# A fused graph block on one core: score matmuls from two float32r parts in 64-row tiles, pairs of slots, and work moved between engines

## The reference

```python
h = relu(layernorm(x))                                  # first block
q, k, v = split(h @ W_qkv + b_qkv)                      # 8 heads of 16
scores = where(adj, q @ k.T / 4, -inf)                  # 512 x 512 per head
x = x + (softmax(scores) @ v) @ W_out + b_out
h = relu(layernorm(x))                                  # second block
zl, zg, v = h @ Wl, h @ Wg, h @ Wv
A_l = zero_diag(relu(cosine(zl, zl)))
A_g = zero_diag(exp(-|zg_i - zg_j|^2 / 2))
K_l, K_g = (row_normalise(A * adj) for A in (A_l, A_g))
x = x + ((0.9 * K_l + 0.1 * K_g) @ v) @ Wo
```

## Time and profile before

| | |
|---|---|
| median of three runs | 993.87 us |
| profiled execution: its own time | 983.95 us |
| profiled execution: span from first to last instruction | 981.9 us |
| TensorE matmuls busy | 876.3 us (89%) |
| TensorE weight loads busy | 496.0 us (51%) |
| VectorE busy | 760.2 us (77%) |
| ScalarE busy | 464.2 us (47%) |
| GpSimd busy | 170.6 us (17%) |
| DMA engines, mean share | 15.9% |
| mean granted TensorE clock | 0.989 |

### The profile page before, as it was taken

How to read it: one execution, slowest core, us unless ns; L and a number is a source line. 1 busy time by engine, 2 the same in 40 slices (tenths; PEclk the granted TensorE clock), 3 DMA queues, 4 the chain that set the end, 5 groups by cost and what they waited for, 6 DMA issues and landing times.

```text
span 981.9 us, 15346 instructions
## 1 busy us (share of the span) xinstructions
PE 876.3 (89%) x4991; PEld 496.0 (51%) x5075; DVE 760.2 (77%) x2461; ACT 464.2 (47%) x833; POOL 170.6 (17%) x224
## 2 busy tenths in 40 slices
PE   1479989999999999999999999999899999999987
PEld 1323345646455554645555464555546464655565
DVE  3767778788787878878688887878887887878465
ACT  1015555354545545364554545454454545455531
POOL 5312030121212021121202112120301212010110
PEclk9999989999999999999999999999999999999998
DMA  1331212030212103030211203021120302100000
GB/s 48 107 97 44 77 48 62 20 101 2 87 33 67 53 28 92 3 103 18 73 47 36 85 9 104 10 76 44 50 71 20 101 2 78 32 12 1 12 11 11
DMA packets 65534, 48.46 MB, mean 49 GB/s; under 512 B 10672, under 2 KB 65456, under 8 KB 65456
## 3 DMA queue, kind: packets, MB, share of 16 engines
q1 hardware_dynamic: 65456, 47.48, 15.9%
HBM read 30.28 MB, written 16.78 MB: 48 GB/s over the span
## 4 chain that ended last, share of the span: by engine, by line
PE 63%; DVE 25%; issue 4%; ACT 3%; SPq 2%; DMA 2%; POOL 1%; POOLq 0%; DVEq 0%; ACTq 0%
PE adj L516 11%; PE pv L509 10%; PE turned L497 8%; PE score L486 8%; PE adj L521 8%; PE turned L496 6%; DVE scrap L706 6%; PE work L527 6%; DVE adj_cos L841 3%; PE work L516 3%; DVE bn_sb L684 2%; DVE x_norm L693 2%; SPq L337 2%; PE work L616 1%; PE work L598 1%
## 5 line engine op out<-in xcount | busy, mean ns | idle before, releaser
L870 ACT ACTIVATE probs_t<-turned 128x512 f32<-128x512 f32 x512 | 306.0, 598 | 263.8 <-PE turned L497 251.3
L706 DVE CUSTOM_DVE_ANT_0 scrap<-score,mask_add 128x512 f32<-128x512 f32 x512 | 338.9, 683 | 30.3 <-PE score L486 29.4
L486 PE MATMUL score<-qk_rows 96*128 96x512 bf16 x512 | 202.6, 398 | 9.5 <-DVE neg_max L706 6.1
L497 PE MATMUL turned<-qk_rows 99*128 99x512 bf16 x512 | 195.5, 382 | 7.7 <-DMA qk_rows<-max_rows 2.9
L496 PE MATMUL turned<-bar_t,ident_b 128*128 128x512 bf16 x428 | 164.0, 383 | 0.8 <-DMA qk_rows<-max_rows 0.8
L509 PE MATMUL pv<-probs_t,v_cols 128*32 128x512 f32 x1024 | 137.3, 609 | 0.0
L486 PEld LDWEIGHTS score<-qk_rows 96*128 96x128 bf16 x512 | 50.2, 99 | 110.6 <-DVE neg_max L706 55.2
L497 PEld LDWEIGHTS turned<-qk_rows 99*128 99x128 bf16 x512 | 50.8, 99 | 58.8 <-issue 1.6
L428 POOL TENSOR_SCALAR var_eps<-moments 128x4 f32<-128x4 f32 x16 | 3.8, 237 | 427.6 <-DVE moments L688 427.6
L521 PEld LDWEIGHTS adj<-z,adj_cos 128*128 128x128 f32 x512 | 67.4, 193 | 10.7 <-DVE adj_cos L729 1.3
L521 PE MATMUL adj<-z,adj_cos 128*128 128x130 f32 x512 | 68.9, 278 | 1.5 <-DVE adj_cos L729 0.8
(11 more groups left out here) (107 smaller groups left out, 1102.3 us busy)
## 6 DMA issues: line engine op xcount, KB each, us to landing
qk_rows<-split_dram SPq DMA_DIRECT2D x384, 64.0 KB, 2.3
split_dram<-split SPq DMA_DIRECT2D x32, 384.0 KB, 2.6
x_sb<-in_x_dram SPq DMA_DIRECT2D x16, 256.0 KB, 2.9
out_dram<-out_sb SPq DMA_DIRECT2D x16, 256.0 KB, 2.3
qk_rows<-max_rows SPq DMA_DIRECT2D x96, 4.0 KB, 1.7
adj_sb<-in_adj_dram SPq DMA_DIRECT2D x1, 256.0 KB, 3.2
wqkv_sb<-in_L_gnn_W_qkv_dram SPq DMA_DIRECT2D x1, 192.0 KB, 2.7
bias_v<-in_L_gnn_b_qkv_dram SPq DMA_DIRECT2D x1, 64.0 KB, 2.8
```

The source lines that it names most:

```text
L486: pe.matmul(score_bank[u % 2][:, :], qk_rows[0:ROWS, b % 2, 0, h, t * P:(t + 1) * P], qk_rows[0:ROWS, b % 2, 1, h, :], start=True, stop=Tr ...
L497: pe.matmul(turned_bank[w % 2][:, :], qk_rows[0:ROWS + 3, b % 2, 1, h, j * P:(j + 1) * P], qk_rows[0:ROWS + 3, b % 2, 0, h, :], start=Fals ...
L706: dve.tensor_tensor_reduce(scrap[:, u % 2, :], score_bank[u % 2][:, :], mask_add[:, u % T, :], -1.0, 3.0e38, ALU.add, ALU.min, neg_max[:, ...
L870: act.activation(probs_t[:, k % 4, w % HG, :], turned_bank[w % 2][:, :], ACT.Exp, scale=SCALE).then_inc(probs_ready.sem, 1)
```

## The change

1. q and k are cut in two float32r parts rather than three bfloat16 ones (`Q_PARTS` 0,0,1 and `K_PARTS` 0,1,0): 48 rows rather than 96, four bytes each. Even heads stand from partition 0, odd heads from partition 64 (`ROW_HALVES`), and the matmuls name that 64-row tile (`tile_position`). GpSimd's two parts are gone; VectorE's residue is the second part. The maximum goes in two float32 rows; TensorE now transposes the maxima themselves, and ScalarE and VectorE each write one part from PSUM.
2. Score tiles and turned tiles are placed two at a time, at even slots: first the mask matmuls of both turned tiles, then score, turned, score, turned. The order of tiles is changed so that neighbouring slots are neighbouring heads.
3. Of every four turned tiles one has no mask matmul. GpSimd multiplies its exponentials, read as int32, by a 0/1 tile (`keep_t`).
4. ScalarE rather than VectorE scales both layer norms (with Relu, from a shift that GpSimd computes in two more small operations), and makes the squared sums of `z` (Square with accumulation, 8 a batch).
5. `col` no longer uses TensorE and ScalarE: the 512 values go to DRAM and return as a broadcast load.
6. `AT` has new slots for nearly all steps, with separate entries for each engine. The next `x` is loaded at slot -28, the parts stored at -7, the rows loaded at -6 and -3.

```diff
-Q_PARTS = (0, 0, 0, 1, 1, 2)
-K_PARTS = (0, 1, 2, 0, 1, 0)
+Q_PARTS = (0, 0, 1)
+K_PARTS = (0, 1, 0)
+ROW_HALVES = (0, 64)
+MASK_BY_PE = (1, 2, 3)
...
+    "hT": (-26,), "q": (-24,), "k": (-21,), "v": (-14,), "max_turn": (16, 32),
+    "pv": (28, 32, 36, 40, 44, 48, 52, 56), "y": (52, 58), "yT": (61,), "attn": (62,), "h2T": (66,),
+    "z": (70, 71, 72, 74), "zgT": (76,), "zlT": (78,), "rbf": (78, 82, 86, 88), "cos": (82, 83, 87, 90),
+    "mix_cos": (95, 97, 98, 99), "mix_rbf": (95, 97, 98, 100),
...
+    "ln_scale": (-27,), "hT_copy": (-26,), "q_hi": (-23,), "k_hi": (-21,), "max_copy": (16, 30),
+    "pv_copy": (41, 56), "yT_copy": (61,), "ln2_scale": (65,), "h2T_hi": (66,), "z_copy": (70, 71, 73, 74),
+    "z_sums": (70, 72, 73, 75), "zgT_hi": (77,), "zlT_hi": (79,), "rbf_exp": (80, 83, 86, 92),
...
+    "qk_store": (-7,), "rows": (-6, -3), "x_next": (-28,), "max_load": (18, 34), "col_store": (74,),
+    "col_load": (75,), "store": (113,),
...
+    def pair(slot):
+        return () if slot % 2 else (slot, slot + 1)
...
+    def score_place(u):
+        p, rest = divmod(u, 2 * T)
+        return 2 * p + rest % 2, rest // 2
...
             def scores(b, u):
-                h, t = divmod(u, T)
+                h, t = score_place(u)
+                row = ROW_HALVES[h % 2]
...
-                pe.matmul(score_bank[u % 2][:, :], qk_rows[0:ROWS, b % 2, 0, h, t * P:(t + 1) * P],
-                          qk_rows[0:ROWS, b % 2, 1, h, :], start=True, stop=True).then_inc(scores_filled.sem, 1)
+                pe.matmul(score_bank[u % 2][:, :], qk_rows[row:row + ROWS, b % 2, 0, h // 2, t * P:(t + 1) * P],
+                          qk_rows[row:row + ROWS, b % 2, 1, h // 2, :], start=True, stop=True,
+                          tile_position=(row, 0)).then_inc(scores_filled.sem, 1)
...
+            def turned_mask(b, w):
+                reached(pe, probs_ready, b, w - 1)
+                if w in by_pe:
+                    pe.matmul(turned_bank[w % 2][:, :], ident_b[:, :], bar_t[:, turned_place(w)[1], :], start=True,
+                              stop=False)
...
+                pe.matmul(turned_bank[w % 2][:, :], qk_rows[row:end, b % 2, 1, h // 2, j * P:(j + 1) * P],
+                          qk_rows[row:end, b % 2, 0, h // 2, :], start=w not in by_pe, stop=True,
+                          tile_position=(row, 0)).then_inc(turned_filled.sem, 1)
...
+                tile = probs_t[:, w // HG % 4, w % HG, :].bitcast(I32)
+                pool.tensor_tensor(tile, tile, keep_t[:, w // HG % T, :], ALU.mult).then_inc(probs_masked.sem, 1)
...
-                if hit := tile_due(s, 0):
-                    scores(*hit)
-                if hit := tile_due(s, LAG):
-                    turned_scores(*hit)
+                for at in pair(s):
+                    if hit := tile_due(at, LAG):
+                        turned_mask(*hit)
+                for at in pair(s):
+                    if hit := tile_due(at, 0):
+                        scores(*hit)
+                    if hit := tile_due(at, LAG):
+                        turned_scores(*hit)
...
+                    pe.transpose(work_bank[0:HALF, 0:P], neg_max[:, g, :],
+                                 ident[:, :]).then_inc(max_turned.sem, 1)
...
+                    for t in range(T):
+                        last = act.activation(x_norm[:, t, :], x_sb[:, t, :], ACT.Relu,
+                                              bias=ln_shift[:, t:t + 1], scale=rstd[:, t:t + 1])
...
+                    for a in range(2):
+                        last = act.activation(z_square[:, t, a * D:(a + 1) * D], z[:, t, a * D:(a + 1) * D],
+                                              ACT.Square, accum_out=square_sum[:, t, a:a + 1])
...
+                    sp.dma_start(col_dram.rearrange("(t p) -> p t", p=P), rbf_bias[:, :],
+                                 allow_slow_non_contiguous=True).then_inc(col_stored.sem, 16)
...
+                    sp.dma_start(col_term[:, :], col_dram.partition_broadcast(P)).then_inc(col_ready.sem, 16)
```

More of the change, by code:

```diff
@@ L8 @@
 BF16 = mybir.dt.bfloat16
+I32 = mybir.dt.int32
 ALU = mybir.AluOpType
@@ L67, in graph_blocks @@
     assert D == P and T == 4 and HG * 32 == P and SLOTS == H * T
+    by_pe = [w for w in range(SLOTS) if w % HG in MASK_BY_PE]
+    by_pool = [w for w in range(SLOTS) if w % HG not in MASK_BY_PE]
     def due(slot, name):
@@ L206, in graph_blocks @@
         ln_rstd = signal("ln_rstd")
+        ln_neg = signal("ln_neg")
+        ln_shifted = signal("ln_shifted")
         ln_done = signal("ln_done")
@@ L278, in graph_blocks @@
         out_stored = signal("out_stored", 1, 16)
[L281 to L289, removed]
+        BANK_READ = {
+            ("max_turn", 0): (max_lo, 1), ("max_turn", 1): (max_lo, 2), ("hT", 0): (hT_ready, 1),
+            ("q", 0): (lo_ready, 1), ("k", 0): (lo_ready, 2), ("v", 0): (v_ready, 1), ("y", 0): (y_ready, 1),
@@ L290, in graph_blocks @@
             ("y", 1): (y_ready, 2), ("yT", 0): (yT_ready, 1), ("attn", 0): (x1_ready, 1),
[L291 to L297 removed]
+            ("h2T", 0): (h2T_split, 1), ("zgT", 0): (zgT_split, 1), ("zlT", 0): (zlT_split, 1),
+        }
+        for t in range(T):
+            BANK_READ["z", t] = (z_ready, t + 1)
+            BANK_READ["cos", t] = (cos_ready, t + 1)
+            BANK_READ["rbf", t] = (rbf_arg_ready, t + 1)
+            BANK_READ["mix_cos", t] = (out_ready, t + 1)
@@ new lines, in bank_turns @@
+        def bank_turns(*stages):
+            turns = sorted((AT[name][nth] + SLOTS * b, order, name, nth, b)
+                           for b in range(B) for order, (name, nth) in enumerate(stages))
+            return [turn[2:] for turn in turns]
+        work_turns = bank_turns(
+            ("max_turn", 0), ("max_turn", 1), ("hT", 0), ("q", 0), ("k", 0), ("v", 0), ("y", 0), ("y", 1),
+            ("yT", 0), ("attn", 0), ("h2T", 0), ("zgT", 0), ("zlT", 0))
+        adj_turns = [
+            bank_turns(*[("cos", m) for m in range(T)], ("mix_cos", 0), ("mix_cos", 2), ("z", 0), ("z", 2)),
+            bank_turns(*[("rbf", m) for m in range(T)], ("mix_cos", 1), ("mix_cos", 3), ("z", 1), ("z", 3)),
+        ]
@@ L298, in work_bank_free, with bank_free @@
+        def bank_free(engine, turns, batch, name, nth=0):
+            place = turns.index((name, nth, batch))
             if place:
-                _, _, name, nth, batch = WORK_TURNS[place - 1]
-                sig, count = WORK_DONE[name, nth]
+                name, nth, batch = turns[place - 1]
+                sig, count = BANK_READ[name, nth]
                 reached(engine, sig, batch, count)
@@ L503, in attend @@
                 ends = (k + 1) * HG
-                reached(pe, probs_ready, b, ends)
+                reached(pe, probs_masked, b, sum(w < ends for w in by_pool))
+                if by_pe:
+                    reached(pe, probs_ready, b, 1 + max(w for w in by_pe if w < ends))
                 if j == 0:
@@ L858, in _, with exponentials @@
             act.wait_ge(s_qkv_loaded.sem, s_qkv_loaded.per * 16)
+            def exponentials(b, w):
+                k = w // HG
+                reached(act, turned_filled, b, w + 1)
+                if w % HG == 0:
+                    reached(act, pv_filled, b, k - 3)
+                act.activation(probs_t[:, k % 4, w % HG, :], turned_bank[w % 2][:, :], ACT.Exp,
+                               scale=SCALE).then_inc(probs_ready.sem, 1)
             for s in slots:
```

367 lines of the change are left out of this document (175 added, 192 removed).

## The result

The changed kernel takes 1046.6 us (median of 4 runs, 1045.9 to 1047.6), the kernel before 994.5 us beside it: ratio of the runs 1.053, 95% interval 1.049 to 1.056. Slower by 5%, where 913 us was forecast and 865 to 985 as the range.

What follows compares the result with a forecast made beforehand. TensorE's instruction stream was taken as the bound. Start 40, filling 30 + 36 + 50, twelve steady batches 624 and tail 122 gave 902 us of span, 913 us as median; own range 875 to 950, wider 865 to 985.

Steps and rivals of the forecast that it cites:

- the paragraph on SyncE: DMA issue: row loads hidden in steady batches, column term without waits, maximum rows' thin margin allowed 0.3 us a batch.
- tile shapes: Score and turned tiles: row halves one after another or a full drain, 1.22 us a pair, median scale 1008 us; chance 0.14.
- coupled pairs: Pairs couple PE and VectorE: idle time grows to 8 us, batch 57 us, median scale 975 us; chance 0.14.
- GpSimd or late rows: GpSimd's int32 multiplication above 5.5 us, or late rows: 980 to 1010 us; chance 0.03.
- TensorE's pair: Score and turned matmuls in two row halves: 0.46 us streaming plus 0.30 in and out, 0.76 a pair, 12.2 a batch.
- Engine sums: Busy time per steady batch: PE 48.9 us, VectorE 40.6, ScalarE 33.4, GpSimd 18.
- The squares: ScalarE: eight squares with accumulation a batch at 0.36 us each, 2.9 us.
- The scalings: ScalarE: eight layer-norm scalings of 128 columns a batch at about 0.28 us each, 2.2 us.
- The steady batch: Twelve batches: PE 48.9 us plus 3.1 idle, 52.0 us against 56.6; 624 us in all, 55 less.
- rival 4: Better than forecast: changes hidden, waits gone, batch 48.5 us, median scale 870 us or below; chance 0.12.
- The clock: Warning sign: a granted clock well below 0.99 would make the whole forecast wrong.
- Filling: First three batches while the overlap fills: 30, 36 and 50 us, against 39.1, 39.6 and 54.2.

Runs made afterwards that it cites:

- e5: Changed kernel, complete, with the column term stored in 16 contiguous bytes per partition and read by VectorE's sum with a four-element step: 893.0 us, ratio 0.904.
- e1: Changed kernel with the column term made as before, by TensorE transpositions and a ScalarE copy, without DMA: 915.9 us, ratio 0.923.
- e4: e1 with all score and turned tiles in the lower 64 partitions, so none run side by side, odd heads left out: 1024.7 us, ratio 1.032.
- e6: e5 without pairs: every slot places its own mask, score and turned tile: 1085.6 us, ratio 1.098.
- e3: Changed kernel with the column store in 16-byte pieces, the term's order left wrong and the product term multiplied by zero: 888.1 us, ratio 0.894.
- e12: e5 with the squared sums of z back on VectorE: 890.5 us, ratio 0.901.
- e7: e5 with TensorE adding the mask to all turned tiles and GpSimd multiplying none: 913.9 us, ratio 0.925.
- e8: Kernel before with only the column term's way through DRAM in 4-byte elements added: 1115.5 us, ratio 1.129.
- e9: Changed kernel storing 128 rather than 512 4-byte elements from the second batch on, product term multiplied by zero: 1009.7 us, one run.

## Why the prediction was wrong, point by point

**The step that failed** is in the paragraph on SyncE: the column term's store and load "have no like row; between 1.7 (small rows) and 6 us each, against five to seven slots, nothing waits". The term was put at nothing, and three things in it were off.
- The store's price: 9.5 us, above the upper end of 6. That bound rested on rows of other, wider transfers, and the four-byte pieces, which I named, got no wider bound for it.
- The sum: VectorE's first sum waits for store plus load, one after the other, 14.2 us. Even by my own ends the two could take 12 us, against five to seven slots of 1.6, 8 to 11 us.
- The cover: 5.9 us. I counted slots at a batch's mean, while these hold less work.

So "nothing waits" became a wait of 8.0 us a batch for TensorE, 128.0 in all. No rival had it; the slow ones were tile shapes, coupled pairs, and GpSimd or late rows. The wait is most of the 1046.6 - 893.0 = 153.6 us that e5 gives back. Most of the rest goes with the clock: PE is busy 50.4 us a steady batch at a granted clock of 0.93, 48.6 in e5 at 1.00, or 21 us in twelve. That e1's 131 us is so near to 128 is partly luck, because e1 also pays 1.6 us a batch for making the term.

**TensorE's pair** was right: 0.75 us against 0.76, halves side by side (e4), about 0.3 for way in and out (e6). `pv`, the one change of tile shape in the trace before, was a good guide to another shape.

**Engine sums** were right where the hole is gone: PE 48.6 us a batch in e5 against 48.9, and in e1 GpSimd 17.7 against 18 and VectorE 41.1 against 40.6. ScalarE's 32.1 in e5 against 33.4 is right by terms that cancel. The squares fit (a square and its accumulator read come every 0.3 us, 0.36 taken). The scalings cost more (0.385 us from start to start, 0.28 taken by a straight line through two longer copies). The exponentials, not in the sum, came out 1.8 us a batch shorter (277.2 us for all against 306.0).

**The steady batch** was forecast at 52.0 with 3.1 idle. Without the hole it is 49.0 with 0.4 idle: rival 4's 48.5 was nearer than the forecast. I kept idle time that had named causes, the layer-norm scaling above all, though the change removes them. I also misread its size: of the 40.1 us, 15.2 are one wait before the first batch, and a steady batch has 1.8 rather than 2.5.

**The clock** fell from 0.99 to 0.93 in the steady batches and came back to 1.00 in e1, e3 and e5: it goes with the hole, and is not a cause beside it.

**Filling.** The first batch was forecast at 30 us and took 39.3. Its maxima were issued at 58.1, 19 us after its first scores rather than 14. In this stretch a projection's three 512-column products take 1.65 us, where three of that width take 0.96 later, as at the lower level of the clock; e1's trace, with the same durations, has a granted clock of 0.55 there. From the maxima to the second batch it took 19.9 us rather than 16. I had put that time on SyncE, whose 24 row loads did take 12.3 us to issue, but no wait of PE for them is among the waits: TensorE is busy for 16.7 of the 18.7 us from 58.1 to 76.8, with matmuls as long. The second batch took 48.9 against 36, with the clock at 0.83. These missing 22 us have nothing to do with the hole: e1 has them too (38.4 and 46.9, 19 us too long). There they are made up by luck, by twelve steady batches of 50.5 us where 52.0 was forecast, 18.5 us in all; this is why e1's 915.9 looks closer to 913 than its parts are.

**VectorE's relief** got no price of its own in the forecast, since TensorE was to be the bound, and e12 shows zero for the squares. The scaling's move took away its wait in the steady batches, but was not run by itself. GpSimd's share of the masks is worth 21 us (e7).

## What to carry to other kernels

Price a DMA by the shape of its pieces, not by its bytes: when a diff says that a transfer is non-contiguous and no row shows such a piece, leave the upper bound open and make the resulting wait a rival. Add up dependent transfers before comparing them with cover, and count cover in the us of those very slots. When one part of a large change costs far more than it can save, undo that part first; here one store's layout hid what the other parts bring.

## What the runs showed of the hardware that was not expected

- A store of 512 separate 4-byte elements to DRAM landed in 9.5 us (8.7 in e8), of 128 such in 7.3 (e9), of 128 pieces of 16 bytes in 1.6 (e3, e5). In all of them the DMA engines' last packet ended within 1.3 us of the issue.
- A VectorE sum of 512 columns went from 0.69 to 1.06 us when one SBUF operand was read with a step of 16 bytes (e5).
- Float32r matmuls of 48 and 50 rows in the two 64-row halves start within 0.01 us of each other and take 0.33 us from one round to the next.
- ScalarE scaled 128 columns from SBUF in 0.48 us by the records, 0.385 from one start to the next, where copies of 512 columns from PSUM took 0.58 to 0.60.
